# A two-block perceiver on one core: the first self-attention reordered, with dense head products

## The reference, cut to what matters

```python
x = x + _L0_attn_ref(_layernorm(x), ...)      # the first self-attention
    xn = _layernorm(x, ln_g, ln_b)
    q, k, v = (split_heads(xn @ W.T) for W in (Wq, Wk, Wv))    # 4 heads of 64
    q = _rmsnorm(q, q_gamma) * SCALE          # over the 64 features of a head
    k = _rmsnorm(k, k_gamma)
    sim = einsum('bhid,bhjd->bhij', q, k)     # 64 x 64 for each batch and head
    out = einsum('bhij,bhjd->bhid', softmax(sim), v)
    return merge_heads(out) @ Wo.T + bo
x = x + _L0_ffn_ref(_layernorm(x), ...)
    h = relu(x @ gate_w1.T + gate_b1)
    g = (h @ gate_w2.T + gate_b2).mean(axis=1)     # 8 mixing weights for each batch
    u = gelu(x @ (W1 + sum_e g_e TW1_e).T + ...)   # the hidden layer, 1,024 wide
    out = u @ (W2 + sum_e g_e TW2_e).T + ...
```

## Time and profile before

| what | value |
| --- | --- |
| three runs | 504.24, 506.49, 506.94 us |
| the profiled execution, its time | 504.44 us |
| its span, first to last instruction | 502.6 us |
| mean granted TensorE clock | 0.983 of full speed |
| TensorE matmul busy | 478.9 us (95%) |
| VectorE, ScalarE, GpSimd busy | 255.7, 235.0, 74.3 us |
| from HBM | 61.84 MB |

### The profile page before, as it was taken

One profiled execution on the slowest core, in us unless ns is written; L12 is line 12 of the kernel. 1 busy time (PEld: TensorE's weight loads), 2 busy tenths in 40 slices (PEclk: granted clock), 3 DMA queues, 4 the chain that ended last, 5 costly groups with the idle time before them and its releaser, 6 DMA issues.

```text
span 502.6 us, 8568 instructions
## 1 busy us (share of the span) xinstructions
PE 478.9 (95%) x3616; PEld 410.9 (82%) x3616; DVE 255.7 (51%) x446; ACT 235.0 (47%) x412; POOL 74.3 (15%) x61
## 2 busy tenths in 40 slices
PE   7999999999999999999897999998999999889997
PEld 6987989899988989899775868984656788778697
DVE  2836222246146131312345895866676566367585
ACT  1737332346245323231033867734787353137772
POOL 2102000000010000000110153546000000004342
PEclk9979999999999999999999999997899999999999
DMA  8647100020620000000096999990000083264000
GB/s 319 235 169 239 38 1 1 1 85 19 234 81 4 1 0 1 1 0 2 1 400 277 333 290 420 409 383 3 1 2 1 3 349 153 85 243 176 0 1 10
DMA packets 12934, 62.51 MB, mean 124 GB/s; under 512 B 1279, under 2 KB 3711, under 8 KB 7008
## 3 DMA queue, kind: packets, MB, share of 16 engines
q1 hardware_dynamic: 10304, 52.17, 27.3%
q0 software_dynamic: 2592, 9.80, 5.6%
HBM read 61.84 MB, written 0.13 MB: 123 GB/s over the span
## 4 chain that ended last, share of the span: by engine, by line
PE 79%; DVE 7%; ACT 4%; POOL 4%; issue 3%; DMA 1%; POOLq 1%; SPq 0%; DVEq 0%; ACTq 0%
PE W L1333 18%; PE W L1294 15%; PE W L1477 8%; PE W L1524 5%; PE W L1597 4%; PE W L1564 4%; PE W L1231 3%; PE W L1275 3%; PE W L1310 3%; POOL w_lo L497 3%; PE W L1614 2%; PE W L1355 2%; POOL small L505 1%; ACT w_hi L553 1%; PE W L1547 1%
## 5 line engine op out<-in xcount | busy, mean ns | idle before, releaser
L1333 PE MATMUL W<-probs_turned_hi,ctx_split_hi 128*128 128x256 f32 x256 | 72.8, 285 | 0.1
L1333 PE MATMUL W<-probs_turned_hi,ctx_split_lo 128*128 128x256 f32 x256 | 72.5, 283 | 0.0
L1333 PE MATMUL W<-probs_turned_lo,ctx_split_hi 128*128 128x256 f32 x256 | 72.4, 283 | 0.0
L875 DVE TENSOR_TENSOR probs_turned_lo<-W,probs_turned_hi 128x512 fp32r<-128x512 f32 x32 | 20.6, 686 | 65.1 <-ACT probs_turned_hi L603 65.1
L1294 PE MATMUL W<-ctx_turned_hi,q_keys_hi 128*128 128x512 f32 x128 | 52.3, 409 | 0.0
L1524 PE MATMUL W<-w_hi,acts 128*128 128x256 f32 x272 | 50.9, 286 | 1.5 <-DVE acts L842 1.0
L1294 PE MATMUL W<-ctx_turned_lo,q_keys_hi 128*128 128x512 f32 x128 | 51.1, 399 | 0.0
L1294 PE MATMUL W<-ctx_turned_hi,q_keys_lo 128*128 128x512 f32 x128 | 51.0, 399 | 0.0
L1333 PEld LDWEIGHTS W<-probs_turned_hi,ctx_split_hi 128*128 128x128 f32 x256 | 49.1, 192 | 0.8 <-DVE probs_turned_lo L875 0.5
L1333 PEld LDWEIGHTS W<-probs_turned_lo,ctx_split_hi 128*128 128x128 f32 x256 | 49.1, 192 | 0.2
L1333 PEld LDWEIGHTS W<-probs_turned_hi,ctx_split_lo 128*128 128x128 f32 x256 | 49.1, 192 | 0.0
(11 more groups left out here) (348 smaller groups left out, 898.4 us busy)
## 6 DMA issues: line engine op xcount, KB each, us to landing
arena<-units_dram SPq DMA_DIRECT2D x22, 1024.0 KB, 10.2
ctxmem<-units_dram SPq DMA_DIRECT2D x16, 1024.0 KB, 12.1
fixed<-units_dram SPq DMA_DIRECT2D x7, 1024.0 KB, 7.0
scr<-ctx_dram POOLq DMA_DIRECT2D x4, 512.0 KB, 3.7
pbuf<-ctx_dram POOLq DMA_DIRECT2D x4, 512.0 KB, 5.6
ctxmem<-ctxT_dram SPq DMA_DIRECT2D x8, 256.0 KB, 11.7
ctxmem<-ctx_dram SPq DMA_DIRECT2D x2, 1024.0 KB, 15.8
scr<-ctxT_dram POOLq DMA_DIRECT2D x3, 512.0 KB, 6.5
```

What stands on the lines that cost most here:

```text
L875: dve.tensor_tensor(PT[1][at], bank(4 + c).rearrange("p (t m) -> p t m", t=4), f32(PT[0][at]), ALU.subtract).then_inc(ev("pl_sb"), 1)
L1333: mm = pe.matmul(ps, CXN[a][:, t, c * P:(c + 1) * P], PT[z][:, t, :], start=(t == 0 and n == 0), stop=(t == KEYT - 1 and n == 2))
```

## The change

The change does the following.

- Keys are projected first (256 columns, bank 2), then queries (bank 4), then values (bank 3). Each has its own square, sum and power: the power on GpSimd is asked for twice, four factors wide (`RSQRT_K`, `RSQRT_Q`).
- The keys get their norm's factors before they are turned. The queries get only the product of the two gammas (`GQK`, a new multiplication of 128 x 64); their factors are applied to the scores.
- The scores are 64 x 64 products, two batches by four heads; two multiplications by the queries' factors take the place of the four copies. Two heads lie side by side on the 128 columns of a turned tile, so that two blocks of probabilities are turned rather than four, and `PA` and its zeros go.
- The values are computed a second time with the batches swapped on the partitions (`VSWAP`), because a head's turned probabilities lie on the partitions of its place in the tile and not of its batch.
- The result is copied to `xT` half by ScalarE and half by VectorE.
- The padding of 14 calls goes, that of 17 becomes 13. The splits of `f1e0` are put elsewhere.
- In the feed-forward layer, the gate's small product stands between the two halves of `f1b`.

```diff
@@ GpSimd
-                src, dst, wide = {RSQRT_QK: (ssq, rqk, 8), RSQRT_PAIR: (ve2, rstd2, 2)}.get(n, (ve, rstd, 1))
+                src, dst, wide = {RSQRT_K: (ssq[:, HA:], rqk[:, HA:], HA), RSQRT_Q: (ssq[:, 0:HA], rqk[:, 0:HA], HA),
+                                   RSQRT_PAIR: (ve2, rstd2, 2)}.get(n, (ve, rstd, 1))
...
-                    pool.memset(PA, 0.0).then_inc(ev("pa_zero"), 1)
@@ ScalarE
-            act.activation(SQ, bank(2), ACT.Square).then_inc(*tick("sq_ready"))
+            act.activation(SQ[:, DIM:], bank(2)[:, 0:DIM], ACT.Square).then_inc(*tick("sqk_ready"))
             act.wait_ge(ev("qkv_ps"), 2)
+            act.activation(SQ[:, 0:DIM], bank(4)[:, 0:DIM], ACT.Square).then_inc(*tick("sqq_ready"))
+            act.wait_ge(ev("qkv_ps"), 3)
             act.copy(vsb[:, :], bank(3)[:, 0:DIM]).then_inc(ev("v_sb"), 1)
-            act.wait_ge(*made("qkT_ps"))
-            act.copy(QKT, bank(4).rearrange("p (t m) -> p t m", t=4)).then_inc(*tick("qkT_sb"))
-            keep_w_hi("f1e0")
+            act.wait_ge(*made("qTA_ps"))
+            act.copy(QKT[:, 0:2, :], bank(7)[:, 0:DIM].rearrange(...)).then_inc(*tick("qTA_sb"))
+            act.wait_ge(*made("kTA_ps"))
+            act.copy(QKT[:, 2:4, :], bank(1)[:, 0:DIM].rearrange(...)).then_inc(*tick("kTA_sb"))
+            act.wait_ge(*made("vA_ps"))
+            act.copy(VSWAP, bank(0)[:, 0:DIM]).then_inc(*tick("vA_sb"))
             act.wait_ge(*made("simA_max"))
             act.activation(SA, SA, ACT.Exp, scale=DH0 ** -0.5).then_inc(*tick("simA_exp"))
+            keep_w_hi("f1e0", [0])
             act.wait_ge(*made("ptA_ps"))
-            act.copy(PTA, bank(7).rearrange("p (t m) -> p t m", t=4)).then_inc(*tick("ptA_sb"))
-            keep_xT(bank(0))
+            act.copy(PTA, bank(7)[:, 0:DIM].rearrange(...)).then_inc(*tick("ptA_sb"))
+            act.wait_ge(*made("pvA_ps"))
+            act.copy(xT[0:DH0], bank(0)[0:DH0, 0:DIM].rearrange(...)).then_inc(*tick("pvA_sbA"))
+            keep_w_hi("f1e0", [1])
@@ VectorE
+            dve.tensor_tensor(GQK, v_("qk_gamma")[:, 0:DH0], v_("qk_gamma")[:, DH0:], ALU.mult).then_inc(ev("gqk_ready"), 1)
...
+            step(dve.tensor_reduce(ssq[:, HA:], SQ[:, DIM:].rearrange(...), AX_X, ALU.add))
+            dve.tensor_scalar(ssq[:, HA:], ssq[:, HA:], 1.0 / DH0, 1e-16, ALU.mult, ALU.max).then_inc(ev("var_ready"), 1)
+            dve.wait_ge(ev("qkv_ps"), 2)
+            dve.wait_ge(*made("sqq_ready"))
+            dve.tensor_tensor(QK[:, 0:DIM]..., bank(4)[:, 0:DIM]..., bc(GQK, 1, HA), ALU.mult).then_inc(*tick("qA_ready"))
+            dve.wait_ge(ev("rstd_ready"), asked[0])
+            dve.tensor_tensor(QK[:, DIM:]..., bank(2)[:, 0:DIM]..., bc(rqk[:, HA:], 2, DH0), ALU.mult).then_inc(*tick("kA_ready"))
+            step(dve.tensor_reduce(ssq[:, 0:HA], SQ[:, 0:DIM].rearrange(...), AX_X, ALU.add))
+            rsqrt(dve.tensor_scalar(ssq[:, 0:HA], ssq[:, 0:HA], 1.0 / DH0, 1e-16, ALU.mult, ALU.max))
             dve.wait_ge(*made("simA_ps"))
-            for b in range(B):
-                for m in range(2):
-                    ins = dve.tensor_copy(sa4[b * NQ:(b + 1) * NQ, :, m, :], bank(5 + m)[...])
+            for m in range(2):
+                ins = dve.tensor_tensor(sa4[:, :, m, :], bank(5 + m)[:, 0:TOK].rearrange(...), bc(rq[:, :, m], 2, NQ), ALU.mult)
...
-            for b in range(B):
-                ins = dve.tensor_tensor(PA[lo:hi, :, lo:hi], SA[lo:hi], bc(srec[lo:hi], 2, NQ), ALU.mult)
-            ins.then_inc(*tick("probsA"))
-            keep_w_lo("f1e0")
+            dve.tensor_tensor(SA, SA, bc(srec, 2, NQ), ALU.mult).then_inc(*tick("probsA"))
+            keep_w_lo("f1e0", [0])
+            dve.wait_ge(*made("pvA_ps"))
+            dve.tensor_copy(xT[DH0:P], bank(3)[DH0:P, 0:DIM].rearrange(...)).then_inc(*tick("pvA_sbV"))
             dve.wait_ge(*made("outA_ps"))
...
             give(norm(x[:, :], hn[:, :], 1e-5))
+            keep_w_lo("f1e0", [1])
             keep_w_lo("f1e1", [0])
@@ TensorE
-            for lo, hi in ((0, 512), (512, 768)):
+            for bk, at in ((2, DIM), (4, 0), (3, 2 * DIM)):
...
-            stay_warm(6, 14)
-            pe.wait_ge(*made("qk_ready"))
-            for t in range(4):
-                mm = pe.transpose(bank(4)[:, t * P:(t + 1) * P], QK[:, t * P:(t + 1) * P], ident)
-            mm.then_inc(*tick("qkT_ps"))
-            pe.wait_ge(*made("qkT_sb"))
-            for h in range(HA):
-                mm = pe.matmul(bank(5 + h % 2)[...], QKT[o:o + DH0, h // 2, :], QKT[o:o + DH0, 2 + h // 2, :], ...)
+            pe.wait_ge(*made("qA_ready"))
+            for t in range(2):
+                mm = pe.transpose(bank(7)[:, t * P:(t + 1) * P], QK[:, t * P:(t + 1) * P], ident)
+            mm.then_inc(*tick("qTA_ps"))
+            for b in range(B):
+                for k in range(KT):
+                    mm = pe.matmul(bank(0)[(1 - b) * NQ:(2 - b) * NQ, 0:DIM], xT[:, k, b * NQ:(b + 1) * NQ],
+                                   wa[:, k, 2 * DIM:], start=(k == 0), stop=(k == KT - 1))
+            mm.then_inc(*tick("vA_ps"))
+            pe.wait_ge(*made("kA_ready"))
+            for t in range(2):
+                mm = pe.transpose(bank(1)[:, t * P:(t + 1) * P], QK[:, DIM + t * P:DIM + (t + 1) * P], ident)
+            mm.then_inc(*tick("kTA_ps"))
+            pe.wait_ge(*made("qTA_sb"))
+            pe.wait_ge(*made("kTA_sb"))
+            for i in range(2):
+                for b in range(B):
+                    for m in range(2):
+                        o, q = slice(m * DH0, (m + 1) * DH0), slice(b * NQ, (b + 1) * NQ)
+                        mm = pe.matmul(bank(5 + m)[q, i * NQ:(i + 1) * NQ], QKT[o, i, q], QKT[o, 2 + i, q], ...)
             mm.then_inc(*tick("simA_ps"))
-            stay_warm(4, 17)
+            stay_warm(4, 13)
             pe.wait_ge(*made("probsA"))
-            for h in range(HA):
-                mm = pe.transpose(bank(7)[:, h * P:(h + 1) * P], PA[:, h, :], ident)
+            for i in range(2):
+                mm = pe.transpose(bank(7)[:, i * P:(i + 1) * P], SA[:, 2 * i:2 * i + 2, :].rearrange(...), ident)
...
-            for h in range(HA):
-                mm = pe.matmul(bank(0)[o:o + DH0, ...], vsb[:, h * DH0:(h + 1) * DH0], PTA[:, h, :], ...)
-            kept_turned(mm)
+            for i in range(2):
+                for b in range(B):
+                    for m in range(2):
+                        v = vsb if m == b else VSWAP
+                        mm = pe.matmul(bank(3 * m)[o, ...], v[o, h * DH0:(h + 1) * DH0], PTA[o, i, q], ...)
+            mm.then_inc(*tick("pvA_ps"))
...
             for hf in range(2):
+                if hf == 1:
+                    pe.wait_ge(*made("hm_ready"))
+                    for k in range(KT):
+                        mm = pe.matmul(bank(2)[:, 0:B * E], c_("ones"), HM[:, k, :], ...)
+                    mm.then_inc(*tick("g_ps"))
                 for k in range(KT):
                     mm = pe.matmul(bank(4 + hf), xT[:, k, :], w[:, k, hf * 512:(hf + 1) * 512], start=(k == 0), stop=False)
             mm.then_inc(ev("units_used"), 1)
-            pe.wait_ge(*made("hm_ready"))
-            for k in range(KT):
-                mm = pe.matmul(bank(2)[:, 0:B * E], c_("ones"), HM[:, k, :], ...)
-            mm.then_inc(*tick("g_ps"))
```

More of the change, by code:

```diff
@@ L946, in _ @@
             step(dve.tensor_tensor(x[:, :], x[:, :], v_("bo"), ALU.add))
-            dve.wait_ge(*made("sq_ready"))
-            step(dve.tensor_reduce(ssq, SQ.rearrange("p (h d) -> p h d", h=8), AX_X, ALU.add))
-            qk4 = QK.rearrange("p (n h d) -> p n h d", n=2, h=HA)
-            rsqrt(dve.tensor_scalar(ssq, ssq, 1.0 / DH0, 1e-16, ALU.mult, ALU.max),
-                  lambda: dve.tensor_tensor(qk4, bank(2).rearrange("p (n h d) -> p n h d", n=2, h=HA),
-                                            bc(v_("qk_gamma").rearrange("p (n d) -> p n d", n=2), 2, HA), ALU.mult))
@@ L953, in _ @@
-            qk8 = QK.rearrange("p (h d) -> p h d", h=8)
-            dve.tensor_tensor(qk8, qk8, bc(rqk, 2, DH0), ALU.mult).then_inc(*tick("qk_ready"))
+            dve.tensor_tensor(GQK, v_("qk_gamma")[:, 0:DH0], v_("qk_gamma")[:, DH0:], ALU.mult).then_inc(ev("gqk_ready"), 1)
+            dve.wait_ge(ev("gqk_ready"), 1)
+            dve.wait_ge(*made("sqk_ready"))
+            step(dve.tensor_reduce(ssq[:, HA:], SQ[:, DIM:].rearrange("p (h d) -> p h d", h=HA), AX_X, ALU.add))
+            asked[0] += 1
@@ L955, in _ @@
+            dve.tensor_tensor(QK[:, DIM:].rearrange("p (h d) -> p h d", h=HA),
+                              bank(2)[:, 0:DIM].rearrange("p (h d) -> p h d", h=HA), bc(rqk[:, HA:], 2, DH0), ALU.mult)\
+                .then_inc(*tick("kA_ready"))
+            step(dve.tensor_reduce(ssq[:, 0:HA], SQ[:, 0:DIM].rearrange("p (h d) -> p h d", h=HA), AX_X, ALU.add))
+            rsqrt(dve.tensor_scalar(ssq[:, 0:HA], ssq[:, 0:HA], 1.0 / DH0, 1e-16, ALU.mult, ALU.max))
             dve.wait_ge(*made("simA_ps"))
@@ new lines, in _ @@
```

(25 more changed lines are left out.)

42 lines of the change are left out of this document (22 added, 20 removed).

## The result

| | before | changed |
| --- | --- | --- |
| runs | 504.24, 506.49, 506.94, 507.35 us | 499.02, 499.08, 500.47, 501.88 us |
| median | 506.72 us | 499.77 us |
| the profiled execution | 504.44 us, span 502.6 | 501.88 us, span 500.1 |
| mean granted clock of it | 0.983 | 0.980 |

The ratio is 0.9881, 95% interval 0.9852 to 0.9909: 4.6 to 7.5 us faster, 6.0 in the middle. The forecast was 3.8 us, 502.7 for the median. (A fourth run of the kernel before moved its median from the 506.49 on which the forecast stood to 506.72.)

What follows compares the result with a forecast made beforehand. The stretch from 250.91 to 275.09 us was taken as latency-bound. 2.84 us up to the output projection plus 0.94 at the gate made 3.8 us off the median of 506.49: 502.7 us, range 500.2 to 505.0.

Steps and rivals of the forecast that it cites:

- The tie of padding and probabilities: Self-attention softmax: 13 padding calls end at 260.5 us, probabilities are ready at 260.53, so the padding costs nothing.
- the covered splits of f1e0: Self-attention: VectorE's split (1.23 us) and ScalarE's (1.05) of these weights fit into waits, adding nothing to the chain.
- the queries' factors off the path: Before the scores: the queries' sum and power run from 254.8 to 256.7 us (257.2 at most), costing nothing.
- the swapped values' product: Self-attention, TensorE: second values product, eight records at 0.215, 1.72 us to 255.77, sets the keys' turn instead of the power.
- The other bound: If the two 64-column halves ran side by side: product 0.86 us, keys' power sets the path, 0.85 us more gain.
- the small products: Self-attention: 16 score records of 64 columns at 0.032 each take 0.78 us; 16 value records add 0.1 us.
- The power of four: Self-attention, keys' and queries' norm factors: the four-wide power takes 1.1 us, between 0.56 one wide and 1.65 eight wide.
- The gate: Feed-forward layer: gate between the halves of f1b lets VectorE start the mixing weights at 274.15, 0.94 us sooner.
- The rival of the late weights: Layer behind: f2e1 lands about 302.6, margin 3.4 us shrinks by 1.2 and holds; if gone, 503.9 us; chance 0.08.
- The rival of the half-speed stretches: Second cross-attention: clock at 1.2 GHz from varying points; median 500.6 or 504.8 us; chance 0.16, half each side.
- The slower rival: Self-attention: with less padding the clock halves at about 252 us for some 10 us; +7, 509.7 us; chance 0.06.

## Why the prediction was right, and where not

**Right: the chain was latency, and its steps.** The tie of padding and probabilities (its 26 records end at 258.74, the probabilities at 258.75), the covered splits of f1e0, the queries' factors off the path, and that the swapped product stands between VectorE's keys and their turn: all as worked out. With the product moved, the keys' turn began 0.5 us earlier.

**Mis-sized: the swapped values' product.** I priced its eight records at 0.215 us one after another, 1.72, and kept 0.86 as the other bound, because "each batch's four records follow one another". They don't hold each other up: records that write opposite halves of the partitions run side by side, 1.08 us for four and 1.09 for eight, 0.63 less than priced. The other bound was off too: at 1.09 and not 0.86, the product still ends after VectorE has the keys (253.63 us; their turn starts at 254.19), so the power does not set the path. The product started 0.2 us later than I had it, so the keys' copy began 0.45 us earlier than forecast (4.86 us after the first projection record, for 5.31). With 0.28 from the scores and less 0.1 for a release, that is the 0.65 us of the table. The reason I gave for my choice was the order of issue, and here the order didn't decide.

**Mis-sized: the small products.** 16 score records took 0.50 us on the chain, for 0.78 forecast; the 64-column loads in front of them are these, in TensorE's timeline of the changed kernel:

```profile
255.15 0.35 PEld L1451 LDWEIGHTS W<-scr 64*64 64x64 f32 x16 [0.76 <-ACT scr L655]
```

0.022 us each. The price from the Trainium skill ("TensorE: Matmul & The Clock Gate", section "LDWEIGHTS (loading the stationary operand)"), 53 ns each, does not hold for such a row of loads on alternating quarters; the nearest row at 0.032 was closer. The value products took 0.70. On the other side, two releases of 0.14 us that I had counted at 0.04 stand before the scores and before the output projection.

**The power of four** took 1.02 us, for 1.1 taken between 0.56 and 1.65. This is its row in the timeline:

```profile
252.16 1.02 POOL L506 TENSOR_TENSOR small<-small,const 128x4 f32<-128x4 f32 x1 [3.90 <-DVE small L958]
```

**The gate** gave 1.04 to 1.06 us, for 0.94, with VectorE's split of f1e1's second half as the last thing before the mixing weights, as forecast (268.27, 1.23 us, in the chain above).

**The rival of the late weights: its margin was wrong by 2 us.** I had f2e1 land at 302.6 in the kernel before, from bytes by time. In fact its load was issued at 288.19, and the DMA issues of the kernel before in 288.1 to 288.4 us (KB each, us to landing) say

```profile
arena<-units_dram SPq DMA_DIRECT2D x1, 1024.0 KB, 16.6
```

so it landed at 304.8, 1.25 us ahead of its split and not 3.4. The margin that was to shrink by 1.2 and hold did not hold: in the changed kernel the split waits 0.3 to 0.5 us. Nothing behind it moves, so the forecast that this costs nothing was right by luck. The sum of bytes took the load as landed once 16.8 MB were in; at 304.8, 54.4 us after the first load at a mean of 325 GB/s, 17.7 MB had moved, so the queue had also moved bytes of loads asked for after it. And asking earlier, which I had taken for safe, is the danger: asked for 20.85 and 20.96 us after the first of the eight, f2e1 came 5 to 6 us late; at 21.4 and more it did not. That another 0.5 us in the self-attention would tip the kernel was in none of my steps.

**The rival of the half-speed stretches was right as a mechanism,** with too small a weight. It is worth up to 3 us in a run, and it is the likely reason why the median fell 0.4 us below the range: 4.57 us are the change up to the first expert, and the rest of the 6.0 is in none of its steps. At the same granted clock the two kernels differ by 4.0 to 4.6 us. The runs of the kernel before fall to the longer stretch in 27 cases of 49, those of the changed kernel in one of ten, as far as their mean clock tells. With the clock held up in both kernels the change is worth 5.0 us by the medians and 4.6 in the stretch that it touches; the interval of the measured 6.0, 4.6 to 7.5, has the first inside it and the second at its lower end.

**The slower rival,** a clock that falls in the self-attention for lack of padding, did not come: no profile of the changed kernel shows it there.

## What to carry to other kernels

Price products that write opposite halves of the partitions as running side by side, whatever their order. When a chain is shortened, look at the loads behind it: read a landing from its own issue and duration, not from bytes by time, and try releasing a buffer later as well as sooner. Before medians are compared to within 1%, look for half-speed stretches in the profile and compare runs at the same mean clock; eight padding calls in one gap were worth 4.2 us here, nearly as much as the whole change.

## What the runs showed that I had not expected

- **Asking for loads sooner made them later.** Asked for 20.85 and 20.96 us after the first of the eight, the three loads had f2e1 landed 35.3 and 36.0 us later. In the profiles of all other runs they were asked for between 21.4 and 25.0 us after the first, and f2e1 landed 29.1 to 31.5 us later, whatever the moment. With the release moved by 2.2 us and nothing else, the layer behind got 2.3 us faster. The first of these three loads took 7.5 us to land when asked for at 270.40, and 4.8 when asked for at 270.70 in the changed kernel. The expectations put the border at the landing of the eighth load, but that is not it: it comes 23.2 to 23.7 us after the first was asked for, and the loads asked for at 21.4 to 23.1 us were not slow. As far as one profile of each kernel tells, the border lies between 20.96 and 21.4 us, and at 20.96 the kernel took 503 to 505 us in only half of its runs. Why is open.
- **A gap of 2.15 us on TensorE cost 3.9 and 6.5 us** (162.9 and 165.5 us from the first scores to the end, for 159.0 with the gap filled). TensorE waited for VectorE and ScalarE, the granted clock fell to 1.2 GHz, and stayed there for 10 or 17 us, although TensorE was busy for 4.00 of 4.00 us in the second window above. The clock fell 0.1 us after the start of the gap in one profile of the changed kernel and 1.5 us after it in the other, so the products before the gap may have a part in it; the run shows only that filling the gap is enough. The Trainium skill says in "TensorE: Matmul & The Clock Gate", section "HAM oscillation — how this bites in real kernels", that waits for a DMA of some 3 to 5 us between bursts of products throttle the clock again; the run with eight padding calls agrees, for a gap shorter than those. Why the stretch is 10 us in one execution and 17 in another was not tried.
